# GpSimd makes some of the probabilities' low halves, queries are copied over both banks, odd steps turn two units earlier, next scores are issued unit by unit

## The chip, the cores and the metric

One core of a Trainium2 chip runs the whole program. The metric is device time in microseconds (us), the median of three runs. The engines are TensorE (PE, with its weight loads as PEld), VectorE (DVE), ScalarE (ACT), GpSimd (POOL) and SyncE (SP), which issues the transfers here.

## The reference, cut

A two-layer block over `x` (16 x 64 x 128) with a context of 16 x 1601 x 128. The change touches only the two cross attentions; the state-space, expert and feed-forward blocks between and behind them stay as they are.

```python
def _L0_xattn_ref(x, latents, Wq, Wkv, Wo, ...):      # x is the context here
    xn = _layernorm(x, ln1_w, ln1_b)
    ln = _layernorm(latents, ln2_w, ln2_b)
    q = ln @ Wq
    k, v = jnp.split(jnp.concatenate([xn, ln], axis=-2) @ Wkv, 2, axis=-1)
    q, k, v = (heads(q), heads(k), heads(v))          # 16 heads of 64
    logits = jnp.einsum('bhld,bhsd->bhls', q * scale, k * scale)
    w = jax.nn.softmax(logits, axis=-1)
    return jnp.einsum('bhls,bhsd->bhld', w, v) ... @ Wo

x = x + _L0_xattn_ref(ctx_1024, _layernorm(x), ...)
x = x + _L0_attn_ref(...);  x = x + _L0_ffn_ref(...)
x = x + _L1_xattn_ref(ctx_1024, _layernorm(x), mask_BxS2_bk0, ...)   # the same with a mask
x = x + _L1_attn_ref(...);  x = x + _L1_ffn_ref(...)
```

## The kernel before, in words

Each attention is one loop of 16 **steps**, one batch element each; an even and an odd step make a **pair**. L0 (no mask) runs from about 73 to 835 us, L1 (masked) from about 1145 to 1897 us. The queries are multiplied by the key weights beforehand, so scores are taken against the normalised context itself (`xT`, 13 tiles of 128 rows, the last of 65) and the products accumulate probabilities times context rows (`x`).

A step has 27 **units**. Unit u belongs to tile u // 2 and one half of the heads; unit 26 is the latents' own keys. For each unit TensorE makes `scores` (three matmuls of 512 columns, L863 to L865) into one of four PSUM banks, ScalarE writes the exponential as f16 (`p_hi`, L1021) and again as f32 **back into the score bank** (L1022), VectorE subtracts the two to get the f16 low half `p_lo` (L1260), and TensorE makes `products` (three matmuls, L891 to L893). Scores run three units ahead (AHEAD), so bank u % 4 is written again as soon as `p_lo` of the unit four before it has been made.

Between the units TensorE does **items** in two further PSUM banks (`aux`), one behind the other: an item starts in a bank when VectorE has freed it (`aux_free`). Even steps: 16 `max` items (one per unit from unit 2 on, L942 and reduced on VectorE, L1202 or L1199), the `turn` (L953, a transpose of the maxima that VectorE makes into the next pair's shift rows, L1218 to L1221, and that SP sends into the queries, L783) and, except in the first step, three `out` items (L901 to L903, divided on VectorE in L1239 and L1245, added up on GpSimd in L759). Odd steps with a pair behind them: four `q` items in units 1 to 4 (the next pair's queries, L922 to L924, 24 matmuls over both banks; ScalarE copies each bank twice, L1008 and L1010, and VectorE makes the low half, L1186), then the maxima and the turn.

Where the items stand is set by two numbers: `TURN_BY = LAST - 4` lets the odd turn stand in unit 22, with `max0` in unit 6 and one maximum a unit. `HOLD = 2` keeps the next step's first three `scores` back to unit 26, where they stand in a row: their first waits for SP's transfer of the shift rows (`shift_in`).

GpSimd's body per step: in even steps the later queries (L1060, L1050), the latents' pair (L1095, L1096); in L0 `context_normal` (roots L281 to L290, 13 tiles L293) and `halves` (a cast L231, a subtraction L233) for the context of two steps on, and then `sums_parted` (L1100, L1050, the high and low halves of the sums); in L1 `sums_parted` and a mask row (L1077); last, in even steps, the outputs (L759, L1126). In the first step of a loop `weights_parted` stands in the place of `sums_parted`. When `halves` is done (`x16_ready`), SP stores the context rows (L215), waits for them to land, loads the next raw context (L189 to L192), makes transposes (L203), loads the rows (`load_x`, L198, 832 KB) and only then sends the shift rows (L783).

The lines that set scores back and place the items:

```python
elif at.has_next and u > LAST - AHEAD + HOLD:
    k = u + AHEAD - STEPS
    for k in range(0 if k == HOLD else k, k + 1):
        scores(k, at.npar, at.half + STEPS, at.n, at.ni)
```

Of the kernel before, what the change touches and what calls it, by code (L numbers as in the profile page):

```python
# [13 lines left out]
ALU = mybir.AluOpType  # L14
# [3 lines left out]
P = 128  # L18
# [107 lines left out]
def cross_attention(nc, glob, name, ctx_dram, mask_dram, w_dram):  # L126
# [12 lines left out]
    with ExitStack() as st:  # L139
# [86 lines left out]
        def halves(pool, n):  # L226
# [6 lines left out]
            pool.tensor_tensor(x16[:, 1, :, :], xt[:, :, :], x16[:, 0, :, :], ALU.subtract).then_inc(x16_ready, 1)  # L233
# [62 lines left out]
        def context_normal(pool, wait, n, par):  # L296
# [233 lines left out]
def attention_loop(nc, glob, name, st, sb, sem, psum, held, mask_dram, context_stats, context_normal):  # L530
# [26 lines left out]
    p_lo = [sb(f"p_lo{k}", [P, HALF], F16) for k in range(RING)]  # L557
    sum_c, sum_l = sb("sum_c", [P, H, 2, L]), sb("sum_l", [P, H, 2, L])
# [35 lines left out]

    def user_before(u):
# [11 lines left out]
    HOLD = 2  # L607
    TURN_BY = LAST - 4
# [116 lines left out]
    def queries_part(a, bank, aux, q, k):  # L725


        src = aux[:, 512 * bank:512 * bank + 512].rearrange("p (c h k l) -> p c h k l", h=2, k=2, l=L)[:, :, :, k, :]
        c = (a % 2) * (NC_ // 2) + bank * (NC_ // 4)
        if k == 0:  # L730
            dst = q[a // 2][0][:, c:c + NC_ // 4, :].rearrange("p c (h l) -> p c h l", l=L)
        else:
            dst = q[:, (a // 2) * HL + c * P:(a // 2) * HL + (c + NC_ // 4) * P].rearrange("p (c h l) -> p c h l", h=2, l=L)
# [27 lines left out]
    with nc.Block() as block:  # L761
# [74 lines left out]
        def _(pe):  # L836
            def scores(u, par, half, b, i):
# [5 lines left out]
                if not (isinstance(half, int) and half + user_before(u) < 0):  # L843
                    pe.wait_ge(p_lo_ready, half + user_before(u) + 1)
# [149 lines left out]
        def _(act):  # L994
            def parts(at, item):
# [1673 lines left out]
```

## Time and profile before

| | us |
|---|---|
| median of three runs | 2065.31 (2063.27 to 2069.19) |
| the profiled execution | 2067.51 |
| its span, first to last instruction | 2065.6 |
| PE busy | 1914.6 (93%) |
| DVE busy | 1682.6 (81%) |
| ACT busy | 1250.5 (61%) |
| POOL busy | 898.2 (43%) |
| L0 loop, a pair: even step, odd step | 47.6, 50.1 |
| L1 loop, a pair: even step, odd step | 47.9, 48.6 |

Busy shares say which engine is near its limit over the whole program, not what holds a given stage. A step's time is read from its windows: where PE is busy for nearly the whole of the window, only what makes PE wait, or gives it less to do, moves the time. Waits are then read on PE's own rows: the bracket behind a row gives the idle time before it and what ended that.

### The profile page before, as it was taken

To read this page: it belongs to the slowest core of one execution; us is meant where nothing else is said; L and a number is where in the kernel's file an instruction comes from. 1 tells how busy PE (TensorE), PEld (TensorE's weight loads), DVE (VectorE), ACT (ScalarE), POOL (GpSimd) and SP (SyncE) were. 2 spreads that over 40 slices of the span, in tenths; PEclk is the share of its full clock that TensorE was granted. 3 is DMA by queue.
4 is the path that set the end of the run, shared out by engine and by line. 5 is a ranking of instruction groups with operands and counts; after the bars stand their busy time and mean duration, and the time that the engine had idled before them with its cause. 6 is when DMAs were issued, how large, how long until landed. Compare 5 with 4: busy or idle time off the path is not lost. (4 is left out here: it accounts for less than half of the span.)

```text
span 2065.6 us, 34989 instructions
## 1 busy us (share of the span) xinstructions
PE 1914.6 (93%) x12326; PEld 1037.9 (50%) x12326; DVE 1682.6 (81%) x3999; ACT 1250.5 (61%) x2237; POOL 898.2 (43%) x951
## 2 busy tenths in 40 slices
PE   7899999999999999899788999999999999998786
PEld 6444544444454544433656545454545454544585
DVE  6889889889989896699666788879797978786657
ACT  4466666665757666444244676867777777776312
POOL 5576565666666652088231424333232323232004
PEclk9899999999999999989998999999999999999898
DMA  4332222222222220132104011211121111110100
GB/s 140 89 105 65 70 67 68 67 68 68 73 73 68 51 67 1 48 115 89 40 1 126 14 38 39 50 39 38 39 59 36 41 39 39 38 30 1 29 1 10
DMA packets 148854, 110.53 MB, mean 54 GB/s; under 512 B 120892, under 2 KB 136232, under 8 KB 148680
## 3 DMA queue, kind: packets, MB, share of 16 engines
q1 hardware_dynamic: 148680, 108.31, 18.8%
q8 instruction: 97, 1.59, 0.3%
q14 instruction: 77, 0.63, 0.1%
HBM read 65.15 MB, written 14.29 MB: 38 GB/s over the span
## 5 line engine op out<-in xcount | busy, mean ns | idle before, releaser
L1260 DVE TENSOR_TENSOR x_p_lo<-x_psum,x_p_hi 128x512 f16<-128x512 f32 (+1 forms) x864 | 583.9, 682 | 110.6 <-ACT x_psum L1022 109.8
L1021 ACT ACTIVATE x_p_hi<-x_psum 128x512 f16<-128x512 f32 (+1 forms) x448 | 268.2, 599 | 260.3 <-PE x_psum L865 210.3
L1021 ACT ACTIVATE x_p_hi<-x_psum,x_bcol 128x512 f16<-128x512 f32 (+1 forms) x416 | 289.7, 696 | 153.9 <-PE x_psum L865 151.9
L891 PE MATMUL x_psum<-x_p_hi,x_x_both 128*128 128x512 f16 (+1 forms) x832 | 317.1, 381 | 30.4 <-DVE x_p_lo L1260 29.5
L863 PE MATMUL x_psum<-x_q,x_xT_both 128*128 128x512 f16 x832 | 316.3, 380 | 3.0 <-DMA x_q<-x_shift_rows 3.0
L892 PE MATMUL x_psum<-x_p_lo,x_x_both 128*128 128x512 f16 (+1 forms) x832 | 315.7, 379 | 0.0
L893 PE MATMUL x_psum<-x_p_hi,x_x_both 128*128 128x512 f16 (+1 forms) x832 | 315.6, 379 | 0.0
L865 PE MATMUL x_psum<-x_q,x_xT_both 128*128 128x512 f16 x832 | 315.6, 379 | 0.0
L864 PE MATMUL x_psum<-x_q,x_xT_both 128*128 128x512 f16 x832 | 315.6, 379 | 0.0
L1199 DVE CUSTOM_DVE_ANT_0 x_junk<-x_psum,x_brow 128x512 bf16<-128x512 f32 (+2 forms) x512 | 279.3, 584 | 8.8 <-PE x_psum L942 6.7
L1202 DVE TENSOR_REDUCE x_mx<-x_psum 128x1 f32<-128x512 f32 (+2 forms) x512 | 276.6, 583 | 2.2 <-PE x_psum L942 1.1
L1022 ACT ACTIVATE x_psum<-x_psum,x_bcol 128x512 f32<-128x512 f32 (+1 forms) x416 | 277.2, 666 | 0.0
L942 PE MATMUL x_psum<-x_xT_both,x_q 128*128 128x512 f16 (+2 forms) x1024 | 264.2, 338 | 10.6 <-DVE x_mx L1202 4.6
L1022 ACT ACTIVATE x_psum<-x_psum 128x512 f32<-128x512 f32 (+1 forms) x448 | 267.4, 597 | 0.0
L1077 POOL TENSOR_SCALAR x_brow<-x_mrow 128x1536 bf16<-128x1536 uint8 x16 | 36.2, 2264 | 393.5 <-DVE x_shift_rows L1221 372.8
L942 PEld LDWEIGHTS x_psum<-x_xT_both,x_q 128*128 128x128 f16 x1024 | 99.6, 97 | 168.0 <-DVE x_mx L1199 56.3
L293 POOL TENSOR_SCALAR x_xt<-x_raw,x_xmean,x_xr 128x127 f32<-128x127 f32 x201 | 161.6, 820 | 17.1 <-DVE x_xr L91 15.4
L891 PEld LDWEIGHTS x_psum<-x_p_hi,x_x_both 128*128 128x128 f16 (+1 forms) x832 | 81.1, 97 | 173.5 <-DVE x_p_lo L1260 83.4
L759 POOL TENSOR_TENSOR x_prod<-x_prod 128x1024 f32<-128x1024 f32 (+3 forms) x56 | 67.1, 1198 | 211.9 <-DVE x_prod L1245 208.6
L893 PEld LDWEIGHTS x_psum<-x_p_hi,x_x_both 128*128 128x128 f16 (+1 forms) x832 | 81.5, 98 | 98.6 <-issue 0.6
L865 PEld LDWEIGHTS x_psum<-x_q,x_xT_both 128*128 128x128 f16 x832 | 81.4, 98 | 98.6 <-issue 0.3
L892 PEld LDWEIGHTS x_psum<-x_p_lo,x_x_both 128*128 128x128 f16 (+1 forms) x832 | 81.6, 98 | 78.2 <-issue 0.3
(486 smaller groups left out, 3609.8 us busy)
## 6 DMA issues: line engine op xcount, KB each, us to landing
x_x_both<-context_rows SPq DMA_DIRECT2D x32, 832.0 KB, 5.3
context_rows<-x_x SPq DMA_DIRECT2D x16, 832.0 KB, 3.5
x_raw<-in_ctx SPq DMA_DIRECT2D x16, 768.0 KB
ssm_c_row<-ssm_bc_rows SPq DMA_DIRECT2D x16, 512.0 KB, 4.2
ssm_b_wide<-ssm_bc_rows SPq DMA_DIRECT2D x7, 512.0 KB, 3.5
x_mrow<-in_mask_BxS_bk SPq DMA_DIRECT2D x16, 200.1 KB
x_Wkv<-in_L_xattn_Wkv SPq DMA_DIRECT2D x4, 512.0 KB, 5.3
x_xT_both<-context_rows SPq DMA_TRANSPOSE x96, 4.0
```

Source lines behind the costliest of these rows:

```text
L863: pe.matmul(out, k_hi, q_hi[0][par][:, chunks, :], start=True, stop=False)
L864: pe.matmul(out, k_hi, q_lo[0][par][:, chunks, :], start=False, stop=False)
L865: pe.matmul(out, k_lo, q_hi[0][par][:, chunks, :], start=False, stop=True).then_inc(s_ready, 1)
L891: pe.matmul(out, v_hi, p_hi[r][rows, :], start=start, stop=False)
L892: pe.matmul(out, v_hi, p_lo[r][rows, :], start=False, stop=False)
L893: pe.matmul(out, v_lo, p_hi[r][rows, :], start=False, stop=stop).then_inc(pv_done, 1)
L942: ins = pe.matmul(aux[:, 512 * bank:512 * bank + w], lhs, xT_hi[at.npar][:, k:k + w], start=True, stop=True)
L1021: act.activation(p_hi[r][rows, :], score[r][rows, :], ACT.Exp, scale=SCORE_UNIT, **bias).then_inc(p_hi_ready, 1)
L1022: act.activation(score[r][rows, :], score[r][rows, :], ACT.Exp, scale=SCORE_UNIT, **bias).then_inc(p32_ready, 1)
L1199: ins = v.tensor_tensor_reduce(junk[:, 512 * bank:512 * bank + w], src, brow[:, w0:w0 + w], 1.0, -3.4e38, ALU.add, ALU.max, m)
L1202: ins = v.tensor_reduce(m, src, AX.X, ALU.max)
L1260: v.tensor_tensor(p_lo[r][rows, :], score[r][rows, :], p_hi[r][rows, :], ALU.subtract).then_inc(p_lo_ready, 1)
```

## The change

1. `BY_POOL` names units whose low half GpSimd makes: in L0 units 10, 13 and 16 of even steps and 8, 11, 14, 17 and 20 of odd ones; in L1 five and seven units. For these ScalarE writes the f32 exponential into one of two SBUF tiles (`p32`) in place of the score bank, GpSimd subtracts, VectorE skips the unit, TensorE waits for GpSimd (`p_lo_pool`) before the products, and the score bank is free as soon as the second exponential has been read out (`p32_ready`).
2. GpSimd's body is put in another order for it: in L0 even steps `sums_parted` stands ahead of `context_normal`, with a low half at tiles 0, 4 and 8; in L0 odd steps low halves stand at tiles 4 and 8, ahead of `halves` and in the middle of its subtraction, the rest behind it and `sums_parted` last. In L1 the low halves stand behind `sums_parted`. A first step has `weights_parted` there.
3. A query item is copied by one instruction of 512 columns over both banks in place of two of 256, on ScalarE and on VectorE alike; both banks count as free when it is done.
4. `TURN_BY = LAST - 6`: the odd turn stands in unit 20, so two maxima each stand in units 6 and 7.
5. `HOLD` is gone: the next step's scores 0, 1 and 2 stand in units 24, 25 and 26, each ahead of the unit's products.

```diff
@@ halves(pool, n, between=None)
+            pool.tensor_tensor(x16[:, 1, 0:FRONT, :], xt[:, 0:FRONT, :], x16[:, 0, 0:FRONT, :], ALU.subtract)
+            between()
+            pool.tensor_tensor(x16[:, 1, FRONT:KT, :], xt[:, FRONT:KT, :], x16[:, 0, FRONT:KT, :], ALU.subtract).then_inc(x16_ready, 1)
...
+    BY_POOL = (((10, 13, 16), (8, 11, 14, 17, 20)), ((9, 11, 13, 15, 17), (8, 10, 12, 14, 16, 18, 20)))[masked]
...
-    HOLD = 2
-    TURN_BY = LAST - 4
+    TURN_BY = LAST - 6
...
@@ scores(u, ...)
-                    pe.wait_ge(p_lo_ready, half + user_before(u) + 1)
+                    v = user_before(u)
+                    if by_pool(par if v >= 0 else 1 - par, v % STEPS):
+                        pe.wait_ge(p32_ready, half + v + 1)
+                    else:
+                        pe.wait_ge(*lows_made(b, v))
...
@@ products(u, at)
-                pe.wait_ge(p_lo_ready, at.half + u + 1)
+                pe.wait_ge(*lows_made(at.b, u))
...
@@ TensorE body
-                    elif at.has_next and u > LAST - AHEAD + HOLD:
-
-                        k = u + AHEAD - STEPS
-                        for k in range(0 if k == HOLD else k, k + 1):
-                            scores(k, at.npar, at.half + STEPS, at.n, at.ni)
+                    elif at.has_next:
+                        scores(u + AHEAD - STEPS, at.npar, at.half + STEPS, at.n, at.ni)
...
@@ ScalarE, a query item
-                for bank in range(2):
-                    act.wait_ge(aux_ready, at.ready(item, bank))
-                    later, src = queries_part(a, bank, at.place(item), later_q, 1)
-                    act.activation(later, src, ACT.Copy, scale=Q_UNIT)
-                    high, src = queries_part(a, bank, at.place(item), q_hi, 0)
-                    act.activation(high, src, ACT.Copy, scale=Q_UNIT).then_inc(hi_ready, 1)
+                act.wait_ge(aux_ready, at.ready(item))
+                later, src = queries_part(a, at.place(item), later_q, 1)
+                act.activation(later, src, ACT.Copy, scale=Q_UNIT)
+                high, src = queries_part(a, at.place(item), q_hi, 0)
+                act.activation(high, src, ACT.Copy, scale=Q_UNIT).then_inc(hi_ready, 2)
...
@@ ScalarE, probabilities
+                whole = score[r]
+                if by_pool(at.par, u):
+                    made = lows_made(at.b, u)[1] - 1
+                    whole = p32[made % 2]
+                    if made > 1:
+                        act.wait_ge(p_lo_pool, made - 1)
...
@@ GpSimd
+            def probability_lows(at, units):
+                for u in units:
+                    made = lows_made(at.b, u)[1] - 1
+                    wait_alone(pool, p32_ready, at.half + u + 1)
+                    low(p32[made % 2][:, :], p_lo[u % RING][:, :], p_hi[u % RING][:, :]).then_inc(p_lo_pool, 1)
...
@@ VectorE, a query item
-                    for bank in range(2):
-                        v.wait_ge(hi_ready, at.n * HI_PARTS + 2 * a + bank + 1)
-                        (hi, src), (lo, _) = (queries_part(a, bank, aux, q, 0) for q in (q_hi, q_lo))
-                        v.scalar_tensor_tensor(lo, src, Q_UNIT, hi, ALU.mult, ALU.subtract).then_inc(aux_free, 1)
+                    v.wait_ge(hi_ready, at.n * HI_PARTS + 2 * a + 2)
+                    (hi, src), (lo, _) = (queries_part(a, aux, q, 0) for q in (q_hi, q_lo))
+                    v.scalar_tensor_tensor(lo, src, Q_UNIT, hi, ALU.mult, ALU.subtract).then_inc(aux_free, 2)
```

VectorE, L0 odd step, from the last query item to the first maxima, before (L1186 is a query's low half, one per bank; L1260 a probability's low half; L1202 a reduction of one bank; L249 context statistics):

```order
L1186 SCALAR_TENSOR_TENSOR x_q<-x_psum,x_q 128x2x128 [waits x0_hi_ready] x2
L1260 TENSOR_TENSOR x_p_lo<-x_psum,x_p_hi 128x512 [waits x0_p32_ready] x2
L1202 TENSOR_REDUCE x_mx<-x_psum 128x1 [waits x0_aux_ready] x2
L1260 TENSOR_TENSOR x_p_lo<-x_psum,x_p_hi 128x512 [waits x0_p32_ready]
L1202 TENSOR_REDUCE x_mx<-x_psum 128x1 [waits x0_aux_ready] x2
```

The same place after (L1233, L1308 and L1249 are the same operations):

```order
L1233 SCALAR_TENSOR_TENSOR x_q<-x_psum,x_q 128x4x128 [waits x0_hi_ready]
L1308 TENSOR_TENSOR x_p_lo<-x_psum,x_p_hi 128x512 [waits x0_p32_ready] x2
L1249 TENSOR_REDUCE x_mx<-x_psum 128x1 [waits x0_aux_ready] x8
L1308 TENSOR_TENSOR x_p_lo<-x_psum,x_p_hi 128x512 [waits x0_p32_ready]
L1249 TENSOR_REDUCE x_mx<-x_psum 128x1 [waits x0_aux_ready] x2
```

One query instruction stands where two stood, and eight reductions (four maxima) follow the low halves of units 6 and 7, where one maximum followed them.

GpSimd, L0 even step, from the context's tiles on, before:

```order
L293 TENSOR_SCALAR x_xt<-x_raw,x_xmean,x_xr 128x127 x12
L231 CAST x_x<-x_xt 128x1664 [waits x0_xt_ready,x0_x_stored]
L233 TENSOR_TENSOR x_x<-x_xt,x_x 128x1664 [waits x0_x_hi_ready]
L1100 CAST x_vo_both<-x_sum_c 128x16x64 [waits x0_sum_out1,x0_prep_done,x0_aux_free,x0_sum_out]
L1050 TENSOR_TENSOR x_vo_both<-x_sum_c,x_vo_both 128x16x64 [waits x0_part_high,x0_prep_done]
```

The same place after (L1127 and the first L1077 belong to the sums, the other L1077 are the probabilities' low halves, the roots stand between the two and are left out of the second piece):

```order
L1127 CAST x_vo_both<-x_sum_c 128x16x64 [waits x0_sum_out1,x0_prep_done,x0_aux_free,x0_sum_out]
L1077 TENSOR_TENSOR x_vo_both<-x_sum_c,x_vo_both 128x16x64 [waits x0_part_high,x0_prep_done]
```

```order
L1077 TENSOR_TENSOR x_p_lo<-x_p_0,x_p_hi 128x512 [waits x0_p32_ready,x0_prep_done,x0_root_steps]
L298 TENSOR_SCALAR x_xt<-x_raw,x_xmean,x_xr 128x127 x4
L1077 TENSOR_TENSOR x_p_lo<-x_p_1,x_p_hi 128x512 [waits x0_p32_ready,x0_prep_done]
L298 TENSOR_SCALAR x_xt<-x_raw,x_xmean,x_xr 128x127 x4
L1077 TENSOR_TENSOR x_p_lo<-x_p_0,x_p_hi 128x512 [waits x0_p32_ready,x0_prep_done]
L298 TENSOR_SCALAR x_xt<-x_raw,x_xmean,x_xr 128x127 x5
L231 CAST x_x<-x_xt 128x1664 [waits x0_xt_ready,x0_x_stored]
L234 TENSOR_TENSOR x_x<-x_xt,x_x 128x1664 [waits x0_x_hi_ready]
```

The sums have moved ahead of the roots, and three low halves, each with a wait for ScalarE, stand among the tiles and ahead of the cast and the subtraction. On TensorE the scores of the next step (their first with the wait for `shift_in`) have moved from behind all products but the latents' to ahead of the products of units 24, 25 and 26.

## Rows read from the trace of the kernel before

**Rows 1.** Windows, one L0 odd step: us, PE, PEld, DVE, ACT, POOL busy, clock, DMA.

```profile
411.40:461.50 50.10, 47.66 (x306) 23.69 (x305) 46.30 (x99) 34.24 (x71) 32.05 (x39) 1.00 0.24 70
```

**Rows 2.** Waits of PE over the whole span: us in total, times, longest.

```profile
PE x_psum L891 <- DVE x_p_lo L1260: 29.5, 50, 3.1
...
PE x_psum L953 <- DVE x_m L1211: 4.6, 14, 0.4
```

**Rows 3.** Timeline of PE, L0 odd step, products(1), queries, products(6): start, us, row, [idle].

```profile
416.41 0.39 PE L891 MATMUL x_psum<-x_p_hi,x_x_both 128*128 128x512 f16 x1 [0.94 <-DVE x_p_lo L1260]
...
417.54 0.23 PE L922 MATMUL x_psum<-x_lnT_hi,x_qk_hi 128*128 128x128 f16 x1 [0.31 <-DVE x_sum_l L1225]
...
418.84 0.22 PE L924 MATMUL x_psum<-x_lnT_hi,x_qk_lo 128*128 128x128 f16 x1
...
420.19 0.22 PE L922 MATMUL x_psum<-x_lnT_hi,x_qk_hi 128*128 128x128 f16 x1
...
420.80 0.22 PE L924 MATMUL x_psum<-x_lnT_hi,x_qk_lo 128*128 128x128 f16 x1
...
426.93 0.22 PE L924 MATMUL x_psum<-x_lnT_hi,x_qk_lo 128*128 128x128 f16 x1
...
429.61 0.39 PE L891 MATMUL x_psum<-x_p_hi,x_x_both 128*128 128x512 f16 x1 [0.52 <-DVE x_p_lo L1260]
```

**Rows 4.** Timeline of ACT, the same stretch.

```profile
419.64 0.60 ACT L1021 ACTIVATE x_p_hi<-x_psum 128x512 f16<-128x512 f32 x1
420.11 0.62 ACT L1022 ACTIVATE x_psum<-x_psum 128x512 f32<-128x512 f32 x1
421.06 0.38 ACT L1008 ACTIVATE x_prod<-x_psum 128x256 f32<-128x256 f32 x1 [0.33 <-PE x_psum L924]
```

**Rows 5.** Timeline of DVE, the same stretch: the low half of unit 7.

```profile
429.86 0.69 DVE L1260 TENSOR_TENSOR x_p_lo<-x_psum,x_p_hi 128x512 f16<-128x512 f32 x1 [0.30 <-ACT x_psum L1022]
```

**Rows 6.** Lines by shape, 120 to 800 us: count, busy us, mean ns.

```profile
L1202 DVE TENSOR_REDUCE x_mx<-x_psum 128x1 f32<-128x512 f32 x224 | 153.9, 687 | 2.2 <-PE x_psum L942 1.1
L1202 DVE TENSOR_REDUCE x_mx<-x_psum 128x1 f32<-128x384 f32 x112 | 61.4, 548 | 0.0
...
L1050 POOL TENSOR_TENSOR x_q<-x_prod,x_q 128x512 f16<-128x512 f32 x28 | 31.5, 1154 | 0.0
```

**Rows 7.** Timeline of PE and DVE, end of an L0 even step: products(24), out1's division.

```profile
503.89 1.02 DVE L1245 TENSOR_TENSOR x_prod<-x_psum,x_rec 128x384 f32<-128x384 f32 x2
...
505.57 0.39 PE L891 MATMUL x_psum<-x_p_hi,x_x_both 65*128 65x512 f16 x1 [0.47 <-DVE x_p_lo L1260]
```

**Rows 8.** Timeline of POOL, ACT and SP, the same L0 even step.

```profile
472.85 10.42 POOL L293 TENSOR_SCALAR x_xt<-x_raw,x_xmean,x_xr 128x127 f32<-128x127 f32 x13
...
485.05 3.34 POOL L233 TENSOR_TENSOR x_x<-x_xt,x_x 128x1664 f16<-128x1664 f32 x1
...
485.66 0.59 ACT L1022 ACTIVATE x_psum<-x_psum 128x512 f32<-128x512 f32 x1
...
494.52 0.53 SPq L198 DMA_DIRECT2D x_x_both<-context_rows  x1
496.61 0.68 SPq L783 DMA_DIRECT2D x_q<-x_shift_rows  x1
```

**Rows 9.** DMA issues, 488 to 502 us: KB each, us from issue to landing.

```profile
x_x_both<-context_rows SPq DMA_DIRECT2D x1, 832.0 KB, 6.0
```

**Rows 10.** Timeline of SP and PE, start of the L0 loop: the shift rows right behind the load.

```profile
67.93 0.72 SPq L783 DMA_DIRECT2D x_q<-x_shift_rows  x1
...
72.33 0.39 PE L863 MATMUL x_psum<-x_q,x_xT_both 128*128 128x512 f16 x1 [2.52 <-DMA x_q<-x_shift_rows]
```

**Rows 11.** Timeline of POOL and DVE, end of the first L0 step, beside `weights_parted`.

```profile
107.77 4.09 POOL L1050 TENSOR_TENSOR x_vo_clo<-x_vo_both,x_vo_chi 128x2064 f16<-128x2064 f32 x1
...
108.51 3.62 DVE L1221 TENSOR_TENSOR x_shift_rows<-x_shift,x_shift_rows 8x256 f16<-8x256 f32 x1
```

**Rows 12.** Windows, the stretch behind that wait; columns as in Rows 1.

```profile
112.60:116.00 3.40, 3.21 (x8) 1.19 (x9) 3.40 (x12) 0.43 (x1) 3.25 (x2) 0.50 0.50 111
```

More of the change, by code:

```diff
@@ L224, in wait_alone, with halves @@
             eng.wait_ge(sem, value)
-        def halves(pool, n):
+        def halves(pool, n, between=None):
             if not (isinstance(n, int) and n == 0):
@@ L232, in halves @@
             wait_alone(pool, x_hi_ready, n + 1)
-            pool.tensor_tensor(x16[:, 1, :, :], xt[:, :, :], x16[:, 0, :, :], ALU.subtract).then_inc(x16_ready, 1)
+            if between is None:
+                pool.tensor_tensor(x16[:, 1, :, :], xt[:, :, :], x16[:, 0, :, :], ALU.subtract).then_inc(x16_ready, 1)
+                return
+            pool.tensor_tensor(x16[:, 1, 0:FRONT, :], xt[:, 0:FRONT, :], x16[:, 0, 0:FRONT, :], ALU.subtract)
+            between()
+            pool.tensor_tensor(x16[:, 1, FRONT:KT, :], xt[:, FRONT:KT, :], x16[:, 0, FRONT:KT, :], ALU.subtract).then_inc(x16_ready, 1)
         x_step = [None]
@@ L294, in normal_tile, with context_normal @@
                                      ALU.subtract, ALU.mult)
-        def context_normal(pool, wait, n, par):
+        def context_normal(pool, wait, n, par, among=lambda j: None):
             if not (isinstance(n, int) and n == 0):
@@ L557, in attention_loop @@
     p_lo = [sb(f"p_lo{k}", [P, HALF], F16) for k in range(RING)]
+    p32 = [sb(f"p32_{k}", [P, HALF]) for k in range(2)]
     sum_c, sum_l = sb("sum_c", [P, H, 2, L]), sb("sum_l", [P, H, 2, L])
@@ L593, in attention_loop, with by_pool, lows_made @@
     part_high, sum_parted, vo_parted = sem("part_high"), sem("sum_parted"), sem("vo_parted")
+    p_lo_pool = sem("p_lo_pool")
+    BY_POOL = (((10, 13, 16), (8, 11, 14, 17, 20)), ((9, 11, 13, 15, 17), (8, 10, 12, 14, 16, 18, 20)))[masked]
+    POOL_EACH = sum(len(x) for x in BY_POOL)
+    def by_pool(par, u):
+        return u in BY_POOL[par]
+    def lows_made(b, u):
+        if u < 0:
+            b, u = b - 1, u + STEPS
+        pool = (b // 2) * POOL_EACH + (len(BY_POOL[0]) if b % 2 else 0) + sum(k <= u for k in BY_POOL[b % 2])
+        return (p_lo_pool, pool) if by_pool(b % 2, u) else (p_lo_ready, b * STEPS + u + 1 - pool)
     def user_before(u):
@@ L723, in wait_alone, with queries_part @@
         eng.wait_ge(sem, value)
[L725 to L729 removed]
+    def queries_part(a, aux, q, k):
+        src = aux.rearrange("p (c h k l) -> p c h k l", h=2, k=2, l=L)[:, :, :, k, :]
+        c = (a % 2) * (NC_ // 2)
         if k == 0:
[L731 removed]
+            dst = q[a // 2][0][:, c:c + NC_ // 2, :].rearrange("p c (h l) -> p c h l", l=L)
         else:
[L733 removed]
+            dst = q[:, (a // 2) * HL + c * P:(a // 2) * HL + (c + NC_ // 2) * P].rearrange("p (c h l) -> p c h l", h=2, l=L)
         return dst, src
@@ L1141, in body @@
             def body(at):
+                lows = list(BY_POOL[at.par])
                 if at.has_next:
@@ L1150, in body, with some_lows, among @@
                     pair(at.i)
-                if at.has_next2 and not masked:
-                    context_normal(pool, wait_alone, at.b + 2, at.par)
-                    halves(pool, at.b + 2)
+                def some_lows():
+                    probability_lows(at, lows[:1])
+                    del lows[:1]
                 if at.first and at.par == 0:
                     weights_parted()
-                else:
+                elif masked or at.par == 0 or not at.has_next2:
+                    sums_parted(at)
+                if at.has_next2 and not masked:
+                    def among(j):
+                        if j in ((0, 4, 8), (4, 8))[at.par]:
+                            some_lows()
+                    context_normal(pool, wait_alone, at.b + 2, at.par, among)
+                    if at.par:
+                        some_lows()
+                    halves(pool, at.b + 2, some_lows if at.par else None)
+                probability_lows(at, lows)
+                if at.has_next2 and not masked and at.par:
                     sums_parted(at)
@@ L1258, in body @@
                     rows = slice(0, TAIL if j == CT else P)
-                    v.wait_ge(p32_ready, at.half + u + 1)
-                    v.tensor_tensor(p_lo[r][rows, :], score[r][rows, :], p_hi[r][rows, :], ALU.subtract).then_inc(p_lo_ready, 1)
+                    if not by_pool(at.par, u):
+                        v.wait_ge(p32_ready, at.half + u + 1)
+                        v.tensor_tensor(p_lo[r][rows, :], score[r][rows, :], p_hi[r][rows, :], ALU.subtract).then_inc(p_lo_ready, 1)
                     if u == 1 and not (at.first and at.par == 0):
```

3 lines of the change are left out of this document (2 added, 1 removed).

## The prediction, made before the changed kernel ran

> **What bounds the kernel now.** I read the windows of the loops first, then the waits of TensorE, then the timelines where it waits. In an L0 odd step TensorE is busy for 47.66 of 50.10 us at clock 1.00, VectorE for 46.30 [rows 1]. So the loops are bound by TensorE, and of an odd step 2.4 us at most can be won by taking waits away. Those waits are nearly all for VectorE: 29.5 us for low halves in 50 places and 4.6 us ahead of the turn in 14 [rows 2], some 34 of 2067 us. Everything else in the change can only put new waits on TensorE. The question is thus whether the relief of VectorE lands where TensorE waits, and what waits come in.
>
> TensorE waits for low halves ahead of products(1) (0.94 us), products(6) (0.52) [rows 3] and products(24) (0.47) [rows 7]. Of these units none is in GpSimd's table, which begins at unit 8 and ends at 20. Its 4 to 6 us less for VectorE per step fall where TensorE doesn't wait.
>
> The sums start from the profiled execution, 2067.5 us, which lies 2.2 over the median.
>
> **Part 1, queries over both banks.** Before, one query's first matmul starts at 417.54 and the next query's at 420.19 [rows 3]: 2.65 us, which is only TensorE's own work (24 query matmuls and the unit's six), since one bank is copied while the other is written. After, nothing is copied until both banks are written, and nothing is written until both are copied. The cycle: 1.30 from the first to the last matmul's start (417.54 to 418.84 [rows 3]); 0.26 until ScalarE starts (420.80 [rows 3] to 421.06 [rows 4]); two copies of 128x512, for which the exponentials of that size stand, 0.47 from start to start and 0.60 [rows 4]; VectorE's low half, like that of a probability, 0.69 [rows 5]; some 0.05 on each side of it. That is 3.42, and TensorE has 2.65 of work in it: 0.77 lost per hand-over. There are three hand-overs in an odd step, and 14 such steps (seven in each loop): 3 x 14 x 0.77 = **+32**. Fewer instructions on ScalarE and VectorE save nothing here, as neither bounds this stretch. Bounds: 20 (the two copies at 0.40 each) to 40.
>
> **Part 2, from the queries to doubled maxima.** The last query's last matmul starts at 426.93, products(6) at 429.61 [rows 3], 2.68 later. ScalarE's next exponentials came 0.80 after a query's last matmul (418.84 [rows 3], 419.64 [rows 4]); after, they come at 0.26 + 2 x 0.47 = 1.20, so products(6) at 3.08. The first maximum, now ahead of products(6), fills that gap. The second can't start: VectorE first makes the low half of unit 7, which started at 429.86 [rows 5], 2.93 after, now 3.33 and to 4.02, and then reduces a bank in 0.687 and the other in 0.548 [rows 6]: the banks come free at 4.7 and 5.2, where TensorE is done with products(6) at 3.7. It loses 1.0 and 0.3 there, 0.7 ahead of products(6), and an estimated 0.4 at the third and fourth maximum, together 2.4, against 0.7 before (start to start; the row shows 0.52 of it as idle [rows 3]): +1.7. In L1, with longer exponentials, I take +2.0 as an estimate. 7 x 1.7 + 7 x 2.0 = **+26**. Lower bound 0, if VectorE, freed of a low half later, and the shorter list of items behind give it back.
>
> **Part 3, next scores not held.** Scores 0', 1', 2' reuse the banks of units 24, 25 and 26, hence wait for their low halves. In even steps the low half of unit 24 stands behind out1's division (1.02 us, and then 0.47 idle ahead of products(24) [rows 7]). That wait stays, now ahead of scores 0'. The low half of unit 26 stands behind out2's division in the same way, and scores 2' no longer stand behind the latest products: an estimated +0.65 in each of 14 even steps, **+9** (bounds 0 and 1.02 each, 14).
>
> **Part 4, the odd turn in unit 20.** It takes the turn's wait (4.6 / 14 = 0.33 [rows 2]) and about 0.4 that VectorE's shift rows cost ahead of products(24) out of 14 odd steps: **-10** (bounds -11 and 0).
>
> **Part 5, GpSimd's order and the shift rows.** In the L0 even step GpSimd begins the ninth of 13 tiles at 472.85 + 8/13 x 10.42 = 479.3 and is done with the subtraction at 485.05 + 3.34 = 488.4 [rows 8], 9.1 us. After, the low half of unit 16 stands ahead of that tile. Its f32 exponential is ready at 485.66 + 0.59 = 486.25 [rows 8]; the low half takes 1.15, as the same operation on queries does [rows 6]; then 9.1: 496.5, 8 us later than before. SP, whose queue is in order, issued the load 6.1 after the subtraction (494.52 [rows 8]), so now at 502.6, and the shift rows behind it at about 503.2 in place of 496.61 [rows 8]. The load lands 6.0 after its issue [rows 9], at 508.6. Behind a load the shift rows were waited for from 67.93 to 72.33, 4.4 [rows 10]: 507.6. Scores 0', no longer held, are wanted where products(24) now start, at 505.57 [rows 7]. So TensorE waits 2.0 to 3.0; I take 2.5 in five even steps, 12.5. In six odd steps, where the subtraction is cut by the low half of unit 17, the same working gives about 1.0, 6. Together **+18.5**, from 0 (the shift rows pass the load) to 33 (3.0 in eleven steps). Before, none of this was seen, since the shift rows were sent 9 us ahead of 505.57.
>
> The Trainium skill, page DMA: Bandwidth & Descriptors, section Queues, rings and completion order, says that each DMA engine consumes the descriptors of a queue row in ring order. By that the shift rows can't pass the load that SP issued before them; the 4.4 us of rows 10 agree, and the term would be its upper one.
>
> **Part 6, the rest.** The low halves themselves: GpSimd takes 1.15 where VectorE took 0.69, with three units between the second exponential and its use, so I cost the others at nothing; what hides them is that lead, and without it each costs 0.5. In L1's first step the first low half stands behind the last piece of `weights_parted`, up to 4.10 (such a piece is in rows 11): **+4**, bounds 0 and 5.
>
> **The sum**: 32 + 26 + 9 - 10 + 18.5 + 4 = +79.5, so 2147 on the profiled execution's basis and **2145 us** for the median. Its own range adds the terms' bounds in part: 2110 to 2180.
>
> **Rivals.** *The loss is only the queries'.* The shift rows land in time and the doubled maxima are given back by VectorE's relief: 32 + 9 - 10 + 4 = +35, **2100** (2080 to 2110). For it: both terms rest on places that the trace of before doesn't show. Against: in both the order on an engine says who stands ahead.
>
> *Faster.* VectorE is busy for 46.30 of 50.10 us [rows 1], and every wait in rows 2 is for it. If five low halves of 0.69 less let it run ahead so that it is never late again, and the two-bank copies are hidden in that slack, all 34 us go: **2031**. It decides at a query cycle of 2.65 or less; then term 1 is nothing, and the rest follows VectorE. Against it stand the 1.30 of matmuls, 1.07 of copies and 0.69 of VectorE in a row that can't overlap.
>
> *Worse.* VectorE's shift row instruction took 3.62 us beside a GpSimd subtraction of 4.09 that began before it [rows 11]. After, the odd L0 turn stands beside low halves and sums on GpSimd, so that the shift rows come later by up to 2.1 in 13 odd and even steps, +27: **2172**. And a long idle can cost twice: behind the one of 3.1 us that the same place caused, TensorE ran at granted clock 0.50, 1.2 in place of 2.4 GHz, for 3.4 us [rows 12], which is 1.7 us of work lost. Seven waits of that length would add 12: 2184.
>
> The Trainium skill, page SBUF — State Buffer, section Who interferes with whom, says that a VectorE instruction with two SBUF inputs contends with a GpSimd instruction that reads SBUF, and that who issues first holds the other fully. Rows 11 agree (3.62 beside 4.09). It speaks against this change, which puts three to seven more such GpSimd instructions into a step; the probabilities' low halves on VectorE have one input in PSUM and would not be held.
>
> *It doesn't do what it says*, or its terms cancel: within 6 us (0.3%, about what a measurement of this kernel tells from no change) of 2065.
>
> **How the numbers follow.** The forecast 0.62, only the queries' loss 0.20, faster 0.10, the same 0.03, worse 0.05. The range leaves out the faster and the same case and half of the worst: **2080 to 2185**. Faster by over 0.3% 0.10, within it 0.03, slower 0.87.
>
> **What would show it.** Right: query first matmuls 3.4 us apart, TensorE waiting for VectorE's query low half; waits of over 1 us ahead of the second maximum in odd steps; TensorE waiting for the shift rows in L0; SP's store of the context rows some 8 us later in even steps; odd steps longer by 4 to 5 us, L0 even ones by about 3. Wrong: query pitches near 2.65, or the low halves' waits gone at products(1) and products(24), or TensorE waiting for GpSimd ahead of products, which I cost at nothing.

## The result, and the profile after

| | before | after |
|---|---|---|
| median, us | 2067.25 (2063.27 to 2071.01, 4 runs) | 2219.07 (2216.09 to 2227.53, 4 runs) |
| ratio | | 1.0741 [1.0703, 1.0779] |
| L0 loop, first exponentials of steps 1 to 16 | 728.7 | 841.4 |
| L1 loop, the same | 717.5 | 755.4 |

The kernel became slower by 152 us, where 80 were forecast; the direction was right and the time lies above the range. Of the profiled executions' difference L0 takes 113 us and L1 38.

TensorE's waits in the changed kernel (engine, line and what it waited for: us in total, times, longest) answer to [rows 2]:

```profile
PE x_psum L888 <- DMA x_q<-x_shift_rows: 40.1, 14, 5.2
PE x_psum L947 <- DVE x_q L1233: 29.6, 42, 0.8
PE x_psum L916 <- DVE x_p_lo L1308: 25.8, 35, 2.2
PE x_psum L967 <- DVE x_mx L1249: 19.7, 22, 3.6
...
PE x_psum L888 <- DVE x_p_lo L1308: 9.3, 20, 0.6
PE x_psum L967 <- DVE x_mx L1246: 9.0, 15, 0.9
```

Three of them are new: the shift rows (14 waits), the queries' low half (42 waits, three in each of 14 odd steps) and the maxima. The wait for low halves, which the change was to shorten, is 25.8 us in place of 29.5 for products, with 9.3 more ahead of scores.

Windows of an odd and an even L0 step and of an odd and an even L1 step (us; PE, PEld, DVE, ACT, POOL busy with instructions; clock; DMA share; GB/s), to be read against [rows 1]:

```profile
467.40:526.60 59.20, 52.50 (x326) 25.47 (x324) 44.28 (x93) 33.42 (x65) 40.11 (x47) 0.96 0.20 59
526.60:585.50 58.90, 50.69 (x288) 23.56 (x287) 45.22 (x89) 29.78 (x57) 30.47 (x38) 0.91 0.20 59
1505.60:1560.00 54.40, 49.96 (x322) 24.34 (x320) 37.86 (x100) 37.59 (x65) 24.48 (x26) 1.00 0.14 37
1560.00:1607.00 47.00, 46.08 (x294) 22.91 (x292) 36.30 (x100) 33.52 (x57) 21.34 (x22) 1.00 0.20 42
```

In L1 the clock is full in these steps. Odd L1 steps take 54.4 us where they took 48.6, and the first step of the loop 47.7 where it took 41.2; the other even steps are 0.9 us shorter. In L0 even steps lose as much as odd ones, and the granted clock is below 1.00 in both.

The same stretch as [rows 3], one L0 odd step, TensorE's timeline: queries, then the doubled maxima.

```profile
476.83 0.23 PE L947 MATMUL x_psum<-x_lnT_hi,x_qk_hi 128*128 128x128 f16 x1 [0.31 <-DVE x_sum_l L1272]
...
480.40 0.23 PE L947 MATMUL x_psum<-x_lnT_hi,x_qk_hi 128*128 128x128 f16 x1 [0.76 <-DVE x_q L1233]
...
483.88 0.23 PE L947 MATMUL x_psum<-x_lnT_hi,x_qk_hi 128*128 128x128 f16 x1 [0.68 <-DVE x_q L1233]
...
487.37 0.23 PE L947 MATMUL x_psum<-x_lnT_hi,x_qk_hi 128*128 128x128 f16 x1 [0.68 <-DVE x_q L1233]
...
491.77 0.39 PE L916 MATMUL x_psum<-x_p_hi,x_x_both 128*128 128x512 f16 x1 [0.28 <-DVE x_p_lo L1308]
...
493.36 0.80 PE L967 MATMUL x_psum<-x_xT_both,x_q 128*128 128x512 f16 x2 [0.77 <-DVE x_mx L1249]
```

Queries start 3.48 us apart (480.40, 483.88, 487.37), where they were 2.65 apart.

**The end of an L0 even step**: SP's store, its load and its shift rows, and TensorE's scores 0' that wait for them.

```profile
568.54 0.37 SPq L215 DMA_DIRECT2D context_rows<-x_x  x1
574.12 0.35 SPq L189 DMA_DIRECT2D x_raw<-in_ctx  x1
...
576.75 0.53 SPq L198 DMA_DIRECT2D x_x_both<-context_rows  x1
577.34 0.68 SPq L804 DMA_DIRECT2D x_q<-x_shift_rows  x1
```

```profile
582.13 0.61 PE L888 MATMUL x_psum<-x_q,x_xT_both 128*128 128x512 f16 x1 [5.24 <-DMA x_q<-x_shift_rows]
```

The windows behind such waits: from 524.00 (behind a wait of 2.1 us), the rest of that step, and from 582.00 (behind the wait above).

```profile
524.00:532.20 8.20, 8.06 (x25) 2.51 (x26) 2.77 (x4) 3.55 (x7) 5.20 (x8) 0.58 0.00 0
532.20:575.00 42.80, 39.82 (x246) 19.61 (x245) 39.02 (x75) 25.14 (x47) 27.88 (x34) 1.00 0.13 36
582.00:591.00 9.00, 8.45 (x49) 4.39 (x50) 3.79 (x12) 3.17 (x7) 2.68 (x2) 0.75 0.01 3
```

TensorE is busy for nearly all of the 8.20 us and runs at a mean clock of 0.58, so most of the stretch is at the level of 1.2 GHz.

Not every wait for the shift rows is followed by such a stretch, and not every such stretch follows one. In the L0 loop of the changed kernel the granted clock is low in 13 stretches, 71.7 us together; before it was low in one, for 3.4 us. Eight of the 13 follow a wait for the shift rows (47.8 us). The other five (23.9 us) stand at the start of even steps, behind two waits for VectorE in a row, of some 2.1 and 1.4 us. And behind five of the 13 waits for the shift rows, of 1.3 to 2.2 us, the clock stays at 1.00. One of these (2.2 us, for the shift rows, ends at 174.51), and one of the pairs for VectorE (its second wait ends at 188.06):

```profile
174.60:182.00 7.40, 7.40 (x37) 3.07 (x37) 4.63 (x8) 5.66 (x11) 6.30 (x10) 1.00 0.01 3
188.10:194.00 5.90, 5.90 (x15) 2.15 (x16) 4.45 (x9) 1.44 (x3) 2.20 (x10) 0.50 0.00 0
```

**The start of the same L0 even step**, VectorE and GpSimd:

```profile
533.06 0.72 DVE L261 TENSOR_TENSOR x_xd<-x_xstats 128x13 f32<-128x13 f32 x1
533.70 0.17 DVE L262 TENSOR_TENSOR x_xm<-x_xstats 128x13 f32<-128x13 f32 x1
533.90 2.16 DVE L264 SCALAR_TENSOR_TENSOR x_xmean<-x_xd,x_xstats 128x13 f32<-128x13 f32 x1
535.98 1.05 DVE L265 SCALAR_TENSOR_TENSOR x_xd<-x_xd 128x13 f32<-128x13 f32 x1
537.06 0.17 DVE L267 SCALAR_TENSOR_TENSOR x_xvar<-x_xm,x_xd 128x13 f32<-128x13 f32 x1
537.15 0.68 DVE L1308 TENSOR_TENSOR x_p_lo<-x_psum,x_p_hi 128x512 f16<-128x512 f32 x1
537.75 1.55 DVE L271 TENSOR_SCALAR x_xrv<-x_xvar 128x13 f32<-128x13 f32 x1
```

```profile
533.89 2.13 POOL L1077 TENSOR_TENSOR x_vo_both<-x_sum_c,x_vo_both 128x1024 f16<-128x1024 f32 x1
535.96 1.04 POOL L1127 CAST x_vo_both<-x_sum_l 128x1024 f16<-128x1024 f32 x1
537.15 2.12 POOL L1077 TENSOR_TENSOR x_vo_both<-x_sum_l,x_vo_both 128x1024 f16<-128x1024 f32 x1
```

VectorE's statistics on 13 columns take 2.16 and 1.05 us exactly beside GpSimd's sums (533.89 to 536.02, 535.96 to 537.00), and 0.17 where nothing runs there. The low half and the maxima queued behind them on VectorE come late. Counted from start to start of TensorE's matmuls, this step loses 1.46 us ahead of products and 1.61 ahead of a maximum, 3.07 together. It is the mildest of six such even steps: the other five lose 2.3 and 1.6, some 3.9 each.

To add waits up over a loop I took, from the trace, the distance of each matmul's start from the one before it, less its own columns at full clock, and put it down to the row's releaser, or to the clock where the distance is doubled without a wait. These distances are called **by starts** below, and their sums are good to a few us. By that L0 lost 40.6 us before and 155.6 after:

| L0, us lost | before | after |
|---|---|---|
| shift rows (DMA) | 0 | 39.7 |
| distance doubled without a wait (low clock) | 8.7 | 39.6 |
| low halves, products and scores | 24.7 | 30.9 |
| maxima (VectorE) | 0.7 | 20.8 |
| queries' low half | 0 | 20.3 |
| others | 6.5 | 4.3 |

The row of the clock holds other small losses too: before it has 8.7 us, though the granted clock was low for 3.4 us only. What counts is its growth, 31 us. The granted clock agrees, as 71.7 us at half the clock are 36 us of work at most.

### The profile page after: what moved, and what is told of

It reads as the page before. It is cut to its first block and busy times, and to the rows that moved or that the text cites. A ratio compares the mean times of both kernels' runs of the same rounds, so it can differ in the third digit from the quotient of the medians.

```text
span 2215.5 us, 35028 instructions
## 1 busy us (share of the span) xinstructions
PE 1966.5 (89%) x12326; PEld 1040.9 (47%) x12326; DVE 1628.5 (74%) x3775; ACT 1240.8 (56%) x2109; POOL 1088.9 (49%) x1118
## 3 DMA queue, kind: packets, MB, share of 16 engines
q1 hardware_dynamic: 148680, 108.31, 17.4%
## 5 line engine op out<-in xcount | busy, mean ns | idle before, releaser
L1308 DVE TENSOR_TENSOR x_p_lo<-x_psum,x_p_hi 128x512 f16<-128x512 f32 (+1 forms) x704 | 474.2, 683 | 87.6 <-ACT x_psum L1049 87.3
L1077 POOL TENSOR_TENSOR x_p_lo<-x_p,x_p_hi 128x512 f16<-128x512 f32 x160 | 185.1, 1157 | 387.7 <-ACT x_p L1049 386.8
L888 PE MATMUL x_psum<-x_q,x_xT_both 128*128 128x512 f16 x832 | 321.3, 386 | 49.5 <-DMA x_q<-x_shift_rows 40.1
L916 PE MATMUL x_psum<-x_p_hi,x_x_both 128*128 128x512 f16 (+1 forms) x832 | 321.2, 386 | 32.0 <-DVE x_p_lo L1308 25.8
L889 PE MATMUL x_psum<-x_q,x_xT_both 128*128 128x512 f16 x832 | 320.4, 385 | 0.0
L890 PE MATMUL x_psum<-x_q,x_xT_both 128*128 128x512 f16 x832 | 320.1, 385 | 0.0
L918 PE MATMUL x_psum<-x_p_hi,x_x_both 128*128 128x512 f16 (+1 forms) x832 | 319.2, 384 | 0.0
L967 PE MATMUL x_psum<-x_xT_both,x_q 128*128 128x512 f16 (+2 forms) x1024 | 275.4, 342 | 37.5 <-DVE x_mx L1249 19.7
L1249 DVE TENSOR_REDUCE x_mx<-x_psum 128x1 f32<-128x512 f32 (+2 forms) x512 | 277.3, 585 | 35.8 <-PE x_psum L967 34.1
L1049 ACT ACTIVATE x_psum<-x_psum 128x512 f32<-128x512 f32 (+1 forms) x384 | 228.9, 596 | 0.0
L1049 ACT ACTIVATE x_psum<-x_psum,x_bcol 128x512 f32<-128x512 f32 (+1 forms) x320 | 212.9, 665 | 0.0
L888 PEld LDWEIGHTS x_psum<-x_q,x_xT_both 128*128 128x128 f16 x832 | 81.9, 98 | 118.2 <-DMA x_q<-x_shift_rows 47.0
L890 PEld LDWEIGHTS x_psum<-x_q,x_xT_both 128*128 128x128 f16 x832 | 82.4, 99 | 101.8 <-issue 5.8
```

Of the source, the lines that this page charges most:

```text
L888: pe.matmul(out, k_hi, q_hi[0][par][:, chunks, :], start=True, stop=False)
L889: pe.matmul(out, k_hi, q_lo[0][par][:, chunks, :], start=False, stop=False)
L890: pe.matmul(out, k_lo, q_hi[0][par][:, chunks, :], start=False, stop=True).then_inc(s_ready, 1)
L916: pe.matmul(out, v_hi, p_hi[r][rows, :], start=start, stop=False)
L918: pe.matmul(out, v_lo, p_hi[r][rows, :], start=False, stop=stop).then_inc(pv_done, 1)
L967: ins = pe.matmul(aux[:, 512 * bank:512 * bank + w], lhs, xT_hi[at.npar][:, k:k + w], start=True, stop=True)
```

## The experiments

**One part undone at a time.** First the queries, copied per bank again, the rest as in the changed kernel:

```diff
-                act.wait_ge(aux_ready, at.ready(item))
-                later, src = queries_part(a, at.place(item), later_q, 1)
...
+                for bank in range(2):
+                    act.wait_ge(aux_ready, at.ready(item, bank))
+                    later, src = queries_part(a, bank, at.place(item), later_q, 1)
...
```

> The changed kernel (2219 us) with its query items copied per bank again; all else stays. Theory: the 42 waits for VectorE's query low half (36.6 us from start to start in the trace of the changed kernel) go, and about 0.4 us in each of 14 transitions to the maxima, so 2219 - 37 - 6 = 2176 us. Rival, in which the stretch is bound by VectorE or ScalarE in any case: the waits only change their name, and the time stays within 10 us of 2219.

Measured 2185.96 us, 33 less than the changed kernel and 10 above the theory. The 42 waits are gone, and the odd L1 step fell from 54.41 to 51.34, 3.1 us each. The L0 loop became 18.5 us shorter and the L1 loop 21.5, together 40 of the 43 expected. The rest lies outside the loops, which the edit doesn't touch: L0 began 4.1 us later in this execution. The shift rows don't come earlier (38 us of waits stay). The theory holds; its rival doesn't.

**Sums behind the context again**, in L0 even steps:

```diff
-                elif masked or at.par == 0 or not at.has_next2:
+                elif masked or not at.has_next2:
                     sums_parted(at)
...
-                if at.has_next2 and not masked and at.par:
+                if at.has_next2 and not masked and (at.par or not at.first):
                     sums_parted(at)
```

> The changed kernel with the sums' halves of L0 even steps put back behind the context's halves and the low halves, as in the kernel before. Theory: GpSimd's sums hold VectorE's context statistics (2.16 and 1.05 us where they took 1.22 and 0.16), and that makes the two waits of 1.5 and 1.6 us early in L0 even steps; both go, 6 x 3 = -18 to -20 us, the waits for the shift rows stay: 2200 us. Rival A, in which these waits come from TensorE's low clock at the step's start: 2219 us, nothing moves. Rival B, in which the earlier sums are what makes the shift rows late: the waits for them (40 us) and the clock lost behind them (31) go as well, 2130 us.

Measured 2214.60 us. The two statistics fell back to 0.18 and 0.17 us and the waits behind them went (by starts, low halves in L0 30.9 to 23.2, maxima 20.8 to 10.7), so the cause is the one named. But the time hardly moved, because a wait that I hadn't foreseen took their place:

```profile
PE x_psum L926 <- POOL x_vo_both L1077: 41.3, 6, 6.9
...
PE x_psum L888 <- DMA x_q<-x_shift_rows: 17.6, 8, 4.6
```

The outputs in units 20 to 24 need the sums' halves. With the low halves in GpSimd's queue these come 6.9 us too late at the old place, in each of six steps. The waits for the shift rows fell as well, from 40.1 to 17.6 us, but the new wait stands ahead of the scores that need them, so this run doesn't rule out rival B; the fourth experiment and the one with the sums alone do. So the changed order on GpSimd isn't free to choose: with the low halves in L0 it is either VectorE's statistics or the outputs.

**Scores held back again:**

```diff
-                    elif at.has_next:
-                        scores(u + AHEAD - STEPS, at.npar, at.half + STEPS, at.n, at.ni)
+                    elif at.has_next and u == LAST:
+                        for k in range(AHEAD):
+                            scores(k, at.npar, at.half + STEPS, at.n, at.ni)
```

> The changed kernel with the next step's three scores held back to unit 26 again. Theory: scores 0' are wanted some 2.7 us later in even steps and 1.3 in odd ones, so of 40 us of waits for the shift rows about 18 stay, the scores' waits for low halves (12.6) go, and 8 us of waits ahead of products(24) come back; the clock follows the waits that are left, so half to all of 31 us stay: 2219 - 22 - 5 - (0 to 15) = 2177 to 2192 us. Rival, in which the transfer only lands when the step's end lets it (it is sent later as well): 2210 to 2219 us.

Measured 2170.92 us, 48 less and 6 below the theory's lower end. 18.8 us of waits for the shift rows stay, as expected. The time at 1.2 GHz in the L0 loop fell from 71.7 us to 38.4, most of it now behind waits for VectorE at the start of even steps. In L1, where the shift rows are never late, a pair takes 100.69 us in place of 101.38: 0.69 is what unheld scores cost by themselves.

**No low half by GpSimd in L0:**

```diff
-    BY_POOL = (((10, 13, 16), (8, 11, 14, 17, 20)), ((9, 11, 13, 15, 17), (8, 10, 12, 14, 16, 18, 20)))[masked]
+    BY_POOL = (((), ()), ((9, 11, 13, 15, 17), (8, 10, 12, 14, 16, 18, 20)))[masked]
```

> The changed kernel without GpSimd's low halves in L0 (VectorE makes them all there; L1 keeps its table, and the order of the sums stays). Theory: the context's halves are done some 8 us earlier, so the shift rows land in time; 40 us of waits and 31 us of low clock behind them go, the statistics' waits (18) stay, and VectorE's later low halves cost up to 8: 2219 - 71 + (0 to 8) = 2148 to 2156 us. Rival on the clock, in which it falls for other waits than those for the shift rows: 2180 us. Rival on the cause, in which the sums or the unheld scores make the shift rows late: 2210 to 2225 us.

Measured 2163.03 us, 56 less. Windows of an even and an odd L0 step, columns as above:

```profile
489.60:539.50 49.90, 46.57 (x293) 22.55 (x291) 45.02 (x92) 29.48 (x56) 29.13 (x37) 1.00 0.23 69
539.50:595.60 56.10, 50.50 (x323) 24.22 (x321) 46.96 (x98) 33.50 (x65) 31.63 (x40) 1.00 0.21 62
```

With the low halves out of GpSimd's way the shift rows come in time (2.1 us of waits left in the L0 loop, by starts) and the clock is 1.00 again (5.0 us at 1.2 GHz in the loop, where there were 71.7). 7 to 15 us more than expected stay. By starts the next scores wait some 6 us more for low halves, which the waits for the shift rows had covered, the turn 2 and the maxima of odd steps 3. Only the last is a place where GpSimd's low halves had helped. The statistics' waits in even steps stay, as the sums do.

**One part alone.** The other way round, each of these is the kernel before with a single part. The queries over both banks:

> The kernel before with the queries' copies over both banks as its one part of the change (no unit by GpSimd, scores held, odd turn in unit 22, sums in their old place). Theory: 42 hand-overs of 0.87 us from start to start, as the trace of the changed kernel has them, and 0.4 us at 14 transitions: 2067 + 37 + 6 = 2110 us. Rival, in which the hand-over only costs because low halves and doubled maxima stand around it: within 15 us of 2067.

Measured 2107.20 us, ratio 1.0193 [1.0171, 1.0214], +40. TensorE's wait, in the same 42 places:

```profile
PE x_psum L947 <- DVE x_q L1234: 29.9, 42, 1.0
```

**Scores held and the odd turn in unit 22**, on top of the third experiment:

```diff
-    TURN_BY = LAST - 6
+    TURN_BY = LAST - 4
```

> The changed kernel with scores held and the odd turn in unit 22 again (the kernel of e3_scores_held, 2171 us, and one part more undone). Theory: the doubled maxima's waits in odd steps go (13.2 us in L1, about 10 in L0), and the waits around the late turn and ahead of products(24) come back with up to 8: 2148 to 2156 us. Rival, in which the queries' late end and not the doubling makes the maxima wait: 2165 to 2175 us.

Measured 2162.02 us, 9 less than with the scores held alone; the theory had 15 to 23. The runs of the two kernels overlap (2157.0 to 2165.5 and 2159.6 to 2177.3), so the odd L1 step is the better measure: it falls by 0.77 us (52.44 to 51.67). By starts, the waits for maxima (1.89 us) and for the query's low half ahead of them (0.29) go, but the wait ahead of products(6) grows from 0.59 to 1.26: the doubling cost 1.5. The waits at the turn and ahead of products(24) grow from 0.32 and 0.16 to 0.57 and 0.58: the early turn had given some 0.7 back.

**Low halves in L1 alone:**

> The kernel before with GpSimd's low halves in L1 as its one part of the change. Theory: the low halves are nearly free but help little, since before's waits stand at units that VectorE still makes: 4.6 us for the first one behind the weights, and up to 10 of before's 20 us of waits in L1 gone: 2057 to 2071 us. Rival, in which VectorE's relief takes all of L1's waits: 2047 us.

Measured 2074.04 us, ratio 1.0032 [1.0022, 1.0042], +7, just outside the theory's range and on the losing side. The first step pays 4.3 us for its first low half behind the weights, and behind that wait the granted clock is low for 6.8 us, so that the step is 6.7 us longer. And the later even steps take 48.26 us in place of 47.90. VectorE and GpSimd there:

```profile
1550.34 0.91 DVE L1257 TENSOR_TENSOR x_shift<-x_const_rows 8x256 f32<-8x256 f16 x1
1551.17 0.67 DVE L1311 TENSOR_TENSOR x_p_lo<-x_psum,x_p_hi 128x512 f16<-128x512 f32 x1
```

```profile
1549.81 1.16 POOL L1079 TENSOR_TENSOR x_p_lo<-x_p,x_p_hi 128x512 f16<-128x512 f32 x1 [2.19 <-ACT x_p L1051]
```

The instruction on the shift, 0.41 us in other steps, takes 0.91: it began beside GpSimd's low half and ended 0.28 us after it (1551.25 and 1550.97). TensorE loses 0.46 us ahead of the low half that follows. So not even the low halves by themselves are free.

**The sums' place alone:**

> The kernel before with the sums' halves of L0 even steps ahead of the context's normalisation as its one part of the change (and the odd steps' subtraction in two pieces). Theory: they hold VectorE's statistics at the step's start as in the changed kernel, 2.9 us in each of seven even steps, and the shift rows come in time, since the context is done only some 3 us later and the scores are held: 2067 + 20 = 2087 us. Rival, in which those waits need the low halves or the unheld scores as well: within 6 us of 2067.

Measured 2094.08 us, ratio 1.0124 [1.0104, 1.0144], +27: no low half and no unheld scores are needed for it. Low halves in L0 make TensorE wait 10 us more than before, maxima 6, and the clock behind takes 8 more, which I had left out. Almost no wait for the shift rows is in this loop (0.6 us), so VectorE's waits alone were followed by the low clock.

**Turn and scores alone:**

> The kernel before with two parts of the change: the odd turn in unit 20 with its doubled maxima, and scores not held. Theory: the doubled maxima cost 1.2 to 1.6 us in 14 odd steps (17 to 23, less 0.4 each for the queries by bank: 12 to 17), scores not held 0.7 in each of 14 pairs (10), the early turn gives back 5 to 10, and the shift rows come in time as no low half delays the context: 2067 + 12 to 22 = 2079 to 2089 us. Rival, in which VectorE only falls behind with GpSimd's low halves or sums beside it: 2060 to 2067 us. Rival for the shift rows (they are late because the scores aren't held): 2067 + 50 or more.

Measured 2091.95 us, ratio 1.0120 [1.0104, 1.0135], +25, 3 above the theory. Some 7 us of waits for the shift rows are in three places only, and 4.9 of them stand ahead of the loop; scores that aren't held don't make them late by themselves.

**A version that beats both.** The statistics' end is also held in the kernel before: its L259 and L262 stand beside GpSimd's additions for the outputs in odd L0 steps, just ahead of products(1), TensorE's longest wait of such a step in [rows 3]. VectorE and GpSimd in the kernel before:

```profile
413.74 1.22 DVE L259 SCALAR_TENSOR_TENSOR x_xmean<-x_xd,x_xstats 128x13 f32<-128x13 f32 x1
...
415.08 0.68 DVE L262 SCALAR_TENSOR_TENSOR x_xvar<-x_xm,x_xd 128x13 f32<-128x13 f32 x1
```

```profile
413.65 1.27 POOL L759 TENSOR_TENSOR x_prod<-x_prod 128x512 f32<-128x512 f32 x1
...
415.00 0.72 POOL L759 TENSOR_TENSOR x_prod<-x_prod 128x256 f32<-128x256 f32 x1
```

```diff
-                    early = [[AGGR]] + [[*range(k, min(k + 4, STATS_PARTS))] for k in range(AGGR + 1, STATS_PARTS, 4)]
+                    early = [[], [], [AGGR]] + [[*range(k, min(k + 4, STATS_PARTS))] for k in range(AGGR + 1, STATS_PARTS, 4)]
```

> The kernel before, with one edit that is no part of the change: in odd L0 steps VectorE ends the context's statistics in units 2 and 3 in place of 0 and 1, behind GpSimd's additions for the outputs and not beside them. Theory (GpSimd instructions hold VectorE's instructions with two inputs in SBUF): the statistics take 1.22 and 0.68 us beside them and some 0.2 each behind them, the low half of unit 1 comes in time, and the waits ahead of products(1) (1.1) and of the first query (0.47) go in some six odd steps: 2067 - 9 = 2058 us. Rival, in which the statistics are long by themselves: the wait moves to a later unit, 2067 us or a few us more.

Measured 2055.94 us, ratio 0.9945 [0.9932, 0.9959]: 12 us faster than the kernel before and 163 faster than the changed one. VectorE's timeline at the place:

```profile
411.37 0.17 DVE L257 TENSOR_TENSOR x_xm<-x_xstats 128x13 f32<-128x13 f32 x1
411.58 0.18 DVE L259 SCALAR_TENSOR_TENSOR x_xmean<-x_xd,x_xstats 128x13 f32<-128x13 f32 x1
411.68 0.44 DVE L260 SCALAR_TENSOR_TENSOR x_xd<-x_xd 128x13 f32<-128x13 f32 x1
412.15 0.17 DVE L262 SCALAR_TENSOR_TENSOR x_xvar<-x_xm,x_xd 128x13 f32<-128x13 f32 x1
```

L259 takes 0.18 us and L262 0.17. The odd L0 step fell from 50.09 to 48.50 us, by the 1.6 that the waits ahead of products(1) and of the first query had cost. Six such steps make 9.5 of the 12 us.

## Why the prediction was right and wrong, by its steps

**Part 1, queries: right.** 0.87 us per hand-over from start to start for 0.77, 36.6 us for 32; alone +40.

**Part 2, doubled maxima: right.** By starts TensorE loses 0.3 us in an odd step for the query's low half ahead of the first maximum, 0.45 (L0) and 0.60 (L1) ahead of products(6), and 1.43 and 1.89 for maxima. That is 2.2 and 2.8, where 0.7 and 0.8 were lost before: +1.5 and +1.9 for the forecast +1.7 and +2.0.

**Part 3, unheld scores: right where nothing else stands there**, 0.69 us a pair in L1 for 0.65.

**Part 4, the early turn: right**, about 0.7 us per odd L1 step by the sixth experiment, for 0.7.

For L1 the parts sum to 33 us (16 + 14 + 4.5 - 5 + 4), and it lost 38; some 3 of the rest is the low clock behind the first step's wait. For L0 they sum to 46, and it lost 113: the failure is in L0, in three terms.

**Part 5, the shift rows, was mis-sized: 39.7 us for 18.5.** The mechanism is the one forecast, in the forecast order, and the fourth experiment shows that the low halves are its cause. But in the step shown the scores were due 8.2 us after the subtraction (576.7 less 568.5), not 9.1; the shift rows landed 5.4 behind the load's issue (582.1 less 576.75), not 5.0; and the store, 3.5 us in most steps, took 5.58 in this one and 4.6 and 4.8 in two others of 12, so that the load was issued 8.2 and not 6.1 behind the subtraction. Even steps waited 3.5 to 5.4 us (the last 1.9) and odd ones 1.5 to 2.4, for 2.5 and 1.0. The slow stores explain some 4.5 us only: three even steps without one still waited 3.5 to 4.0. And two even steps that the forecast hadn't counted, the first (4.9) and the last, add 6.8. The upper bound of 33 was too low as well. That three stores were slower is seen, its cause isn't settled.

One inference in this part doesn't hold. The prediction took from the ring order that the shift rows can't pass the load, and that rows 10 agree. In the step above the load landed later than the shift rows, 6.3 us after its issue, at about 583.1, while TensorE started on the shift rows at 582.13:

```profile
x_x_both<-context_rows SPq DMA_DIRECT2D x1, 832.0 KB, 6.3
```

In the place of rows 10 the load, issued at 67.19, landed 6.8 us later, and TensorE started 1.7 us before that. Elsewhere they keep close: in six of twelve steps TensorE started 0.2 to 0.3 us after the load had landed. No run sent the shift rows ahead of the load, so how much of the wait that order makes is open.

**The clock was put into a rival with 0.05**, at 1.7 us a time, after the one stretch in [rows 12]; the sum had nothing for it. It took some 31 us more in L0, by the times above about two thirds behind the shift rows and one third behind VectorE's waits at the start of even steps. Shift rows by starts, and time at 1.2 GHz, in the L0 loops: before 0 and 3.4 us, without low halves in L0 2.1 and 5.0, with the scores held 17.4 and 38.4, the changed kernel 39.7 and 71.7, with the sums ahead alone 0.6 and 21.5. In the changed kernel all six waits for the shift rows of 3.3 to 5.2 us were followed by a low clock, and two of the seven shorter ones. So a wait of that length has to be priced here with 1.7 to 3.3 us on top (an estimate: half of the time that TensorE then worked at 1.2 GHz).

**The sums' new place was costed at nothing: +27 alone**, and in the changed kernel 22.7 us of waits in six even steps, without the clock. I followed the moved sums on GpSimd's queue and on SP's, not what runs beside them on VectorE. The mechanism did stand among the rivals (the instruction of 3.62 us beside one of 4.09, [rows 11]), but at the odd turn; there nothing happened in the step shown (0.40, 0.40 and 0.44 us), and it struck at the start of even steps, where VectorE has five statistics instructions and the sums had been put. The Trainium skill, page SBUF — State Buffer, section Who interferes with whom, says that a VectorE instruction with two SBUF inputs contends with a GpSimd instruction that reads SBUF. The runs agree where the two inputs lie in SBUF (2.16 beside 2.13, 0.91 beside 1.16), and the probabilities' low halves, with one input in PSUM, were not held: one took 0.68 us at 537.15, where a GpSimd subtraction of 2.12 began. But two inputs aren't the whole condition here: L271, with one, took 1.55 us beside the same subtraction (0.16 in the kernel before), and the turn's last instruction, with two, 0.44 beside a cast. The page told what to look for; I asked it of the turn only.

**Part 6, low halves at nothing: a little too low in L1.** The 4.3 us of the first step were forecast (4). What wasn't is the clock behind them and 0.36 us in each later even step; together they make the +7. TensorE waited for GpSimd's low half only in that first step. The relief of VectorE was also put too high: three to seven low halves of 0.69 us are 2.1 to 4.8 us a step, not 4 to 6, though no term rests on it.

The parts alone add to 40 + 27 + 25 + 7 = 99 us. The other 53 need the low halves in L0, and taking those out of the changed kernel gives 56 back. So the sum closes within the measurement. Low halves in L0 alone weren't run. An estimate by subtraction: with the scores held and the late turn the kernel took 2162, so there they cost some 21 (2162 less 2067, 40, 27 and 7), and the remaining 32 only appear together with unheld scores and the early turn.

## What to carry to other kernels

Where work moves to an idle engine, ask what that engine's queue held behind the place: here three low halves that each wait for ScalarE put off a chain of store, load and a small transfer, and the small transfer held TensorE. Copying two banks by one instruction saves instructions and takes away the overlap between filling one and emptying the other; here the two buffers were the pipeline, and it cost 40 us. And before GpSimd work is moved, look at which VectorE instructions beside its new place read two operands from SBUF.

## What the runs showed of the hardware

A VectorE instruction on 13 columns took 2.16 us beside a GpSimd subtraction of 2.13, and 0.18 with the sums moved away. Of the time at 1.2 GHz in the changed L0 loop, 47.8 us followed waits of 2.0 to 5.2 us for a transfer and 23.9 us pairs of waits for VectorE of some 2.1 and 1.4 us, although TensorE was busy for nearly all of the stretch shown (8.06 of 8.20 us). A small transfer issued behind a load of 832 KB let TensorE start before that load had landed, by about 1 us in the step shown. And the same 832 KB store took 3.5 us in most steps and 4.6 to 5.6 in a few.
